# Output stores regrouped over two queues, and one low-part instruction over whole runs, in a convolutional U-shaped block on one core

## The reference, cut to what matters

```python
def conv3(x, w, stride): ...            # 3x3, padding 1, NCHW
def deconv2(x, w):                      # 2x2 transposed convolution, stride 2
    y = jnp.einsum('nchw,cokl->nohkwl', x, w)
    return y.reshape(n, w.shape[1], 2 * h, 2 * wd)
def basic_block(x, w1, w2, stride=1, ds=None):
    out = relu(conv3(x, w1, stride) * BN_S)
    out = conv3(out, w2, 1) * BN_S
    identity = conv1x1(x, ds, stride) * BN_S if ds is not None else x
    return relu(out + identity)

# v = groupnorm(x), one channel per group; x is (2, 32, 64, 64) float32
v = basic_block(v, e0b0c1, e0b0c2); v = basic_block(v, e0b1c1, e0b1c2); f0 = v      # 64x64
v = basic_block(v, e1b0c1, e1b0c2, stride=2, ds=e1b0ds)
v = basic_block(v, e1b1c1, e1b1c2); f1 = v                                          # 32x32
v = basic_block(v, e2b0c1, e2b0c2, stride=2, ds=e2b0ds)
v = basic_block(v, e2b1c1, e2b1c2)                                                  # 16x16
v = (relu(deconv2(v, dec0w) * BN_S) + f1) * BN_S
v = (relu(deconv2(v, dec1w) * BN_S) + f0) * BN_S
return x + v
```

## Time and profile before

| what | value |
|---|---|
| median of 3 runs | 92.66 us (92.26 to 92.81) |
| the profiled execution, its own time | 92.77 us |
| its span, first to last instruction | 91.0 us |
| mean granted TensorE clock | 0.985 |
| PE, DVE, ACT, POOL busy | 83.7, 64.0, 44.7, 27.6 us |
| written to memory | 1.05 MB |
| last store issued, span's end | 87.4 us, 91.0 us |

### The profile page before, as it was taken

How to read it: one execution, slowest core, us unless ns; L and a number is a source line. 1 busy time by engine, 2 the same in 40 slices (tenths; PEclk the granted TensorE clock), 3 DMA queues, 4 the chain that set the end, 5 groups by cost and what they waited for, 6 DMA issues and landing times.

```text
span 91.0 us, 1549 instructions
## 1 busy us (share of the span) xinstructions
PE 83.7 (92%) x537; PEld 74.2 (82%) x537; DVE 64.0 (70%) x190; ACT 44.7 (49%) x94; POOL 27.6 (30%) x43
## 2 busy tenths in 40 slices
PE   5998999999999999999999999999999989998700
PEld 3666999998777799999977777999999989886500
DVE  5559999799968799646625479999458797333820
ACT  6005214778445065744423359999900199962300
POOL 7300060999920000654440000300892004200330
PEclk9999999999999999999999999999999999999995
DMA  2888820034573013550000000000000000000094
GB/s 24 252 232 307 270 96 0 0 117 105 167 205 131 6 28 102 180 152 6 0 0 0 0 4 0 0 0 0 0 7 0 4 0 0 7 0 0 14 326 122
DMA packets 4183, 6.51 MB, mean 72 GB/s; under 512 B 464, under 2 KB 2000, under 8 KB 4176
## 3 DMA queue, kind: packets, MB, share of 16 engines
q1 hardware_dynamic: 4176, 6.42, 23.4%
HBM read 5.37 MB, written 1.05 MB: 71 GB/s over the span
## 4 chain that ended last, share of the span: by engine, by line
PE 82%; DVE 6%; DMA 4%; issue 1%; SPq 1%; ACT 1%; POOLq 1%
PE psum L828 76%; DMA x_sb<-x_in 4%; PE psum L867 2%; DVE split L724 1%; SPq L416 1%; PE psum L853 1%; PE psum L963 1%; POOLq L165 1%; PE psum L1020 1%; DVE shared L679 1%; DVE split L731 1%; DVE stats L608 1%; DVE moments L623 1%; DVE shared L637 1%; PE psum L860 1%
## 5 line engine op out<-in xcount | busy, mean ns | idle before, releaser
L469 POOL TENSOR_TENSOR odd<-relu,odd 128x363 fp32r<-128x363 f32 x12 | 13.4, 1135 | 16.0 <-ACT odd L544 16.0
L828 PE MATMUL psum<-shared,w_e0b0c 128*128 128x364 f32 x72 | 12.5, 331 | 0.4 <-DVE shared L637 0.4
L828 PEld LDWEIGHTS psum<-shared,w_e0b0c 128*128 128x128 f32 x72 | 12.0, 188 | 0.7 <-issue 0.7
L828 PE MATMUL psum<-shared,w_e0b1c 128*128 128x364 f32 x72 | 12.2, 329 | 0.0
L828 PEld LDWEIGHTS psum<-shared,w_e0b1c 128*128 128x128 f32 x72 | 12.1, 188 | 0.1
L828 PE MATMUL psum<-odd,w_e0b0c 128*128 128x512 f32 x48 | 12.0, 411 | 0.0
L828 PE MATMUL psum<-odd,w_e0b1c 128*128 128x512 f32 x48 | 12.0, 411 | 0.0
L754 DVE SCALAR_TENSOR_TENSOR relu<-psum,inside 128x363 f32<-128x363 f32 (+2 forms) x18 | 8.7, 489 | 3.8 <-PE psum L828 3.6
L828 PEld LDWEIGHTS psum<-odd,w_e0b1c 128*128 128x128 f32 x48 | 9.1, 190 | 2.6
L828 PEld LDWEIGHTS psum<-odd,w_e0b0c 128*128 128x128 f32 x48 | 9.1, 190 | 2.6
L544 ACT ACTIVATE odd<-relu 128x363 fp32r<-128x363 f32 x12 | 6.2, 518 | 7.4 <-DVE relu L754 7.4
(11 more groups left out here) (125 smaller groups left out, 139.0 us busy)
## 6 DMA issues: line engine op xcount, KB each, us to landing
out<-result SPq DMA_DIRECT2D x3, 256.0 KB, 3.1
x_sb<-x_in SPq DMA_DIRECT2D x4, 160.0 KB, 4.3
raw<-e0b0c_in SPq DMA_DIRECT2D x2, 256.0 KB, 4.9
raw<-e0b1c_in SPq DMA_DIRECT2D x2, 256.0 KB, 5.3
raw<-e1b1c_in SPq DMA_DIRECT2D x2, 256.0 KB, 3.0
raw<-e2b1c_in SPq DMA_DIRECT2D x2, 256.0 KB, 2.6
raw<-e1b0c_in SPq DMA_DIRECT2D x1, 448.0 KB, 3.7
raw<-e2b0c_in SPq DMA_DIRECT2D x1, 448.0 KB, 4.0
```

What stands on the lines that cost most here:

```text
L469: pool.tensor_tensor(split_of(piece, 1), fp32_of(piece), split_of(piece, 0).bitcast(F32), ALU.subtract).then_inc(lo_ready, 1)
L828: last = pe.matmul(target, w, moving, start=(first and n == 0), stop=(final and n == len(terms) - 1), skip_group_check=skip)
```

## The change

It does three things. The store of result 2 is issued by ScalarE, behind its last relu, after a wait for the third `result_ready`. SP stores result 0, result 1, results 3 and 4 together, and results 5 to 7 together; its last wait still counts five stores. And the low part of `e2b1c2` is made by one VectorE instruction over the whole runs of both images, 2 x 72 columns with their pads, in place of two over 64 columns each. What it writes in the pads of the low map is read by nothing after it, since `dec0_round` reads the columns of pixels alone.

```diff
 BY_ACT = {3, 7}
+STORES = [(0, 1), (1, 1), (3, 2), (5, 3)]
+STORED_BY_ACT = 2
...
-            stores = [(0, 1), (1, 1), (2, 2), (4, 2), (6, 2)]
-            for first, count in stores:
+            for first, count in STORES:
                 done = range(first + count)
                 sp.wait_ge(result_ready, len([n for n in done if n not in BY_ACT]))
                 if any(n in BY_ACT for n in done):
                     sp.wait_ge(result_added, len([n for n in done if n in BY_ACT]))
                 sp.dma_start(out[:, first:first + count], result[:, first:first + count]).then_inc(stored, 16)
-            sp.wait_ge(stored, 16 * len(stores))
+            sp.wait_ge(stored, 16 * (len(STORES) + 1))
...
             for n in sorted(BY_ACT):
                 act.wait_ge(last_summed, n // 4 + 1)
                 act.activation(result[:, n], last_bank(n), ACT.Relu).then_inc(result_relu, 1)
+            act.wait_ge(result_ready, STORED_BY_ACT + 1)
+            act.dma_start(out[:, STORED_BY_ACT], result[:, STORED_BY_ACT]).then_inc(stored, 16)
...
                     wait_half(dve, piece.index, 0)
+                    if stage.name == "e2b1c2":
+                        first = PITCH[2] + 1
+                        lo, hi = [flat2[:, half, :, first:first + EVEN_RUN[2]] for half in (1, 0)]
+                        last = dve.scalar_tensor_tensor(out=lo, in0=sums, scalar=0.0, in1=hi.bitcast(F32),
+                                                        op0=ALU.max, op1=ALU.subtract)
+                        ins = []
                     for one in range(len(ins)):
                         last = dve.scalar_tensor_tensor(out=los[one], in0=ins[one], scalar=0.0,
                                                         in1=his[one].bitcast(F32), op0=ALU.max, op1=ALU.subtract)
```

## The result

The changed kernel takes 91.83 us, median of 7 runs (91.38 to 92.13); the kernel before, on the same chip, 92.36 us (92.26 to 92.81, 7 runs). The medians differ by 0.53 us. The ratio of the timed runs is 0.9925, 95% interval 0.9904 to 0.9947, which is 0.69 us faster, where 0.13 was forecast. The timed gain is told by this ratio from here on. The profiled execution takes 91.54 us with a span of 89.7, 1.23 us less than the one before. Not all of that is the change's, as the rows show.

A forecast was written before the change was run, and what follows sets the result against it. It took the body as a TensorE-led chain and the last 2.4 us of the drain as bound by transfer engines. Savings 0.05 + 0.08 = 0.13 us off the median 92.66 gave 92.53, rounded to 92.5; range 91.95 to 93.0.

The forecast's parts named there:

- Part 1: Low part of `e2b0c2`'s successor `e2b1c2` in one VectorE instruction of about 0.31 us, not 0.36: 0.05 us saved.
- Part 2: Regrouped stores at the kernel's end, result 2 on ScalarE: 0.08 us saved, bounds 0 and 0.17.
- the case that only the wait counts: ScalarE's store of result 2 goes out at 86.15 us without waiting for its relu; otherwise at 86.30.
- the second dip: Drain at 87.20 to 87.35 us, 164 GB/s with the queue dry; filling it saves 0.08 us, the earlier dip stays.
- I cost the shape at nothing: In the drain, the same bytes moved in pieces of 1, 2 and 3 KB were taken to cost no extra time.
- the last 2.4 us are bound by the engines: After 87.35 us the transfer engines' high share bounds the drain; only the dips belong to the issue.
- a median of three, 92.66: Baseline time of the kernel before; the 0.13 us saving was taken off it to forecast 92.53.
- rows 9: Profile rows of the old drain: engines' share 1.03, 1.12, 0.81 at 381, 333, 246 GB/s after 87.35 us.
- The rival that used this fall: Fewer, wider stores keep 381 GB/s late in the drain, 0.35 us less, giving 92.2; chance 0.12.
- An earlier last store joins a queue that is still full: Last store of the drain: issuing it 0.17 us earlier was not counted as a full gain; 0.08 taken.
- The cold queue: Rival: ScalarE's first store opens a cold queue and loses up to 0.35 us or more, 92.9 to 93.5; chance 0.14.
- The fit: Skill's transfer time, 2.0 us plus bytes at 436 GB/s: last store lands near 90.1, gain about 0.5 us; rejected.
- what was queued ahead: Reason given why the old last store of 256 KB took 3.2 us to land, not the formula's 2.6.

The follow-up runs named there:

- e5: Changed kernel with all stores on SP (0, 1, 2, 3 with 4, 5 to 7), none on ScalarE: ratio 0.9959, first issue to last landing 4.70 us.
- e13: Changed kernel with stores of 0, 1 with 2, 3 with 4, 5 with 6, and 7, all on SP: ratio 0.9932, drain 4.67 us.
- e16: Kernel before with the one low-part instruction, each result stored one place lower in the output's line: ratio 0.9927, drain 4.53 us.
- e6: Changed kernel with its last store of results 5 to 7 cut into 5 and 6 with 7: ratio 0.9992, drain 4.80 us.
- e12: Changed kernel with four stores, all on SP: 0, 1, 2 with 3, 4 to 7: ratio 0.9907, drain 4.57 us.
- e4: Changed kernel with the old groups, 2 with 3 issued by ScalarE and the rest by SP: ratio 0.9990, drain 5.13 us.
- e11: Changed kernel with the identity matrix load moved to ScalarE's queue, so it is used before its store: ratio 0.9942, drain 4.47 us.
- e10: Kernel before with the one low-part instruction, SP issuing the last store only after the first four landed: one run, 94.08 us, drain 6.94 us.
- e9: Changed kernel with four stores of two results each, 0-1, 2-3, 4-5, 6-7, all on SP: ratio 0.9969, drain 4.82 us.
- e1: Kernel before run and profiled again without any edit: ratio 1.0007, first issue to last landing 5.14 us.
- e17: Kernel before with the one low-part instruction and the result tile 1 KB further in on-chip memory: ratio 1.0006, drain 5.15 us.

## Why the prediction was wrong

**Part 1 was right.** 0.31 us for the instruction, 0.05 us on the path, in full, as worked out from the earlier trace rows.

**Part 2 had the times right and the step that carried the sum wrong.** SP's last issue came 0.18 us sooner (0.17 forecast), ScalarE's store went out at 0.67 us after the first (86.15, the time named for the case that only the wait counts, is 0.68), the second dip was filled and the first stayed. The step that failed is "I cost the shape at nothing", and with it the reading that the last 2.4 us are bound by the engines and so can't shrink. The new groups alone are worth 0.43 us (e5), the second queue alone nothing (e4), and both together 0.67. In the records: the five old stores keep an engine busy for 3.21 us, the new ones for 2.90, by the sum of the records over 16 engines, 0.31 less; the engines stand idle within the drain for 0.39 before and 0.18 after, 0.21 less; and the landing follows the last byte by 0.69 before and 0.53 after, 0.16 less. That is 0.68 against the 0.67 of the stretch and the forecast of 0.08. Of these terms the idle time is the one that the forecast costed: with the new groups the second queue fills 0.22 us of it (e5 against the changed kernel), not 0.08. Together with part 1 it is 0.72 us, and the timed runs show 0.69 (interval 0.49 to 0.89). The forecast time has a second miss: it was taken off a median of three, 92.66, where seven runs give 92.36. This 0.30 us of the 0.67 between 92.5 and 91.83 is the baseline's and nothing that the change did. That put the measured time outside the range; off 92.66 even the full 0.69 us would have given 91.97, just inside.

**The sign of it stood in rows 9.** 333 GB/s at a share of 1.12 is 110 ns a piece against 89 just before. I read "share above 1" as the engines' bound and so as unchangeable, and put the excess down to the memory or to uneven ends. The share says that an engine is busy, not that its work must take so long. The rival that used this fall gave 92.2 and had a chance of 0.12. It was the nearest, and half its reason was right: three stores of 2 KB pieces on each other are slow, but only from even KB. From odd KB three of them in a row run at 87 ns (e13, e16), so the gain doesn't need wider pieces. The changed groups both break the row of equal widths and start at 3 and 5 KB; either seems to be enough, the odd starts by e13 and e16, the broken row by e6 (its last 2 KB store is from an even KB and at 88 ns) and e12. Which of the two did it in the changed kernel is not separated.

**"An earlier last store joins a queue that is still full"** was right for the old groups (e4: 0.15 us earlier, nothing gained) and wrong for the new ones (e5 against the changed kernel: 0.19 us earlier, 0.24 gained). With fast pieces the last store has less to wait for: its first byte comes 1.05 us after its issue in the changed kernel and 1.10 in e5, against 1.38 before and 1.46 in e4.

**The cold queue** did not happen: no slow piece on ScalarE's queue (49 ns for 1 KB, as on SP's), first bytes after 1.03 us whether it had been used or not (e11).

**The fit.** The Trainium skill ("DMA: Bandwidth & Descriptors", section on the anatomy of one DMA) gives 2.0 us plus bytes at 436 GB/s for transfers that GpSimd issues. The prediction left this condition out; all stores here go out from SP and ScalarE. By it the last store of 384 KB would land after an estimated 2.9 us, and it took 2.7; for the last store of 256 KB it gives 2.6, and 3.2 was measured in the kernel before and 2.2 in e16. So it was 0.2 to 0.4 us too long once the slow pieces were gone. The prediction put its miss on the old store down to "what was queued ahead"; e16 has the same stores queued ahead and lands after 2.2, so most of the miss was the slow pieces and the later landing.

**What stays open.** Why pieces of 2 KB written from even KB behind each other are slow, and why they peak in the third store, no trace here shows; the write addresses' pattern in the memory is a guess. That the output's own start is even is not shown: the parity is counted from it. e6 has a ratio of 0.9992 where its stretch would give 0.996; its late landing is part of it, the rest isn't explained. The delay from the last byte to the landing ranges from 0.40 us (e16) to 0.79 (e10). It is 0.63 or more in every profile where a 2 KB store from an even KB is last, but for e9 (0.55), and below 0.60 in all others; in e10 that store had drained fast and alone. Why, no run shows.

## What to carry to other kernels

Read share and rate of a drain together and turn them into the time of one piece, 16 x share x bytes / rate; if it grows within one size, an earlier issue may gain nothing and the stores' pattern may, as here. Where stores to one output follow each other, try another cut of the same slabs, before adding a queue: here it was enough that 2 KB pieces did not all start at multiples of 2 KB in a line of 8 KB. Other sizes and pitches were not tried in this way. And count times from a point behind the start: two executions of one kernel differed there by 0.33 us, half of what this change is worth.

## What the runs showed of the hardware

- 2 KB pieces at a pitch of 8 KB, written from even KB of the output in store after store: 87 and 97 ns in the first and second store and 132 to 133 in the first half of the third (before, e1); from odd KB 85 to 90 in every half (e13, e16). Moving the reading side by 1 KB changes nothing (e17: 136 in that half). Alone, an even one takes 86 (e10).
- Without that pattern a piece takes 48 ns for 1 KB, 87 for 2, 123 for 3. 4 KB pieces, from an even KB behind a 2 KB store from an even one, took 173 in their first half and 160 in the second (e12).
- A store issued by ScalarE goes out while its relu still runs (issue 85.55, relu to 85.67), its issue takes 0.35 to 0.37 us. Its first bytes seem to wait for the store ahead: they begin 1.69 to 1.71 us after the first issue whether it was issued at 0.67 or at 0.82 (e4).
